# Row scores over 64 contraction rows on two halves of the array, and a tap buffer of its own in the convolution

## The chip, the cores and the metric

The kernel runs on one core of a Trainium2 chip. The metric is device time in microseconds (us) of one execution. Before the change it is 1879.77 us, the median of three runs (1877.68 to 1879.78).

## The reference

Two transformer layers with modulated layer norms run over 4 batches of 1024 rows of 256 values, all in float32. The first layer is a gated long convolution and a feed-forward part with binarised weights. The second is grouped attention and a mixture of two experts. Cut to what matters here:

```
up = u @ in_w + in_b                         # 768 channels
uc = depthwise convolution of up, 3 taps, + short_b
x0, x1, v = uc[:, :256], uc[:, 256:512], uc[:, 512:]
vx = v * x1                                  # then the long convolution of vx, times x0, @ out_w
...
q, k = rope(h @ Wq), rope(h @ Wk)            # 16 query heads, 4 key heads, 64 values each
scores = q k^T / 8, causal mask              # per head 1024 x 1024
out = softmax(scores) @ v
```

## The kernel before, in words

The program is written by hand for each engine; every engine runs its own list of instructions and waits on semaphores. After a setup it handles the 4 batches one after another with the same code. There is no planner: the order on each engine is the order of the loops, and transfers are issued mostly by SyncE (SP).

**Attention.** The float32 operands are split into a high part and a low part (`fp32r`). `qhh` holds the high part of a head's queries twice, in partitions 0 to 63 and 64 to 127. `khl` holds the high part of the keys in partitions 0 to 63 and their low part in 64 to 127. So one matmul over 128 contraction rows gives q_high times (k_high + k_low). The missing q_low times k_high comes from `q2` and `k2`, which hold q_low and k_high in partitions 0 to 63. Their partition 64 holds the negated row maxima and ones, so that the maximum is subtracted by the same matmul of 65 rows.

A head needs its row maxima before its exponentials. `score_rows(u, i)` (L591) computes the scores of 128 query rows of head u against all keys up to the diagonal, in PSUM: (i+1)*128 columns, in one matmul where they fit in 512 and else in two, each with its own weight load. `row_maxima` (L1239, VectorE) reduces them. Eight such tiles make a head: 12 matmuls and 4608 columns. `turn_maxima` (L598) turns the maxima into a row, ScalarE copies it (L927), and SP copies it into `q2` (L1678).

The main loop (L787 to L798) runs over 16 heads of 12 blocks (c, j). In a block TensorE issues `score_cols` (L611, L613, and on diagonal blocks the causal mask L617), then the row tiles that `rows_at` gives, then `values` of four blocks ago (L631, L632, L634). Row tiles 4 to 7 of the next head stand at blocks 0 to 3, one in each, and row tiles 0 to 3 of the head after it at blocks 8 to 11, one in each. Head 1 is computed in head 0, two tiles in each of blocks 0 to 3. Head 0 has its row tiles ahead of the loop. ScalarE takes two exponentials of each block (L942, L943), VectorE or GpSimd the low part (L1249, L1509). PSUM banks 2 to 7 go round among score blocks and row tiles.

**Convolution stage.** For six channel tiles in `E_ORDER` (v0, x1 of 0, v1, x1 of 1, x0 of 0 and 1), TensorE projects (`up_rows`, L450) and ScalarE writes the first tap (L976). GpSimd corrects two edge columns (L1534) and VectorE adds the other two taps (L1327, L1330). There is one buffer `x1` for both x1 tiles. So the second x1 tile (step n == 3) may be written only when v0 has been multiplied with the first; GpSimd does that at n == 1 (L1537). VectorE multiplies v1 with the second x1 tile at n == 3 (L1335). `gated_rows` transposes the products on TensorE (L642), and `spectra` (L661) goes on from them.

GpSimd fills constants for attention (L1556 to L1563) between the last layer norm of the stage before and the first rotation `rotate(0)` (L1516).

Of the kernel before, what the change touches and what calls it, by code (L numbers as in the profile page):

```python
# [60 lines left out]
def rows_at(u, n):  # L61

    if u == 0 and n < 4:
        rows = [(1, 2 * n), (1, 2 * n + 1)]
    elif n < 4:
        rows = [(u + 1, AHEAD + n)]
    else:
        rows = [(u + 2, n - 8)] if n >= 8 else []
    return [(w, i) for w, i in rows if w < HEADS]
# [17 lines left out]
        "w1_split": 2, "x_done": 1, "tap_made": 1, "edge_done": 6, "gates_mixed": 1, "bias_added": 6, "y_pool": 3,  # L87
        "causal_made": 1, "rope_done": 9, "v_done": 4, "low_pool": 112, "x_loaded": 16,
        "gates_loaded": 16, "first_rows0": 64, "first_cols": 64, "first_rows1": 64, "m_loaded0": 128,
# [39 lines left out]
def adaln_hyena_binffn_gqa_moe(nc, d, out, gate_scratch, kf_scratch, q_scratch, k_scratch, inverse_scratch, scratch):  # L129
    es = ExitStack()  # L130
    with es:
# [94 lines left out]
        with ExitStack() as a:  # L226
            with ExitStack() as a3:
                oT = sb("oT", [P, HEADS * HD // P, L], F32, a3)
                qhh = sb("qhh", [P, QRING, L], F32R, a3)
                q2 = sb("q2", [HD + 1, 2, L], F32R, a3)  # L230
                khl = sb("khl", [P, 2, L], F32R, a3)
                k2 = sb("k2", [HD + 1, 2, L], F32R, a3)
                vhi = sb("vhi", [P, KV, NT, HD + 1], F32R, a3)
                vlo = sb("vlo", [P, KV, NT, HD + 1], F32R, a3)
                psplit = sb("psplit", [P, PRING, 2, HALF], F32R, a3)
                pT = sb("pT", [P, FRING - 1, HALF], F32, a3)
                causal = sb("causal", [P, P], F32R, a3)
                mx = sb("mx", [P, 2, NT], F32, a3)
                nm = sb("nm", [P, 2, NT], F32, a3)
                nmr = sb("nmr", [NT, 2, P], F32R, a3)  # L240
                den = sb("den", [P, 2, NT], F32, a3)
                rden = sb("rden", [P, 2, NT], F32, a3)
# [58 lines left out]
        def load_next(dma, h):  # L301

            cols = slice(h * HALF, (h + 1) * HALF)
            one = flat_split(2 * h + 1)[32:HD]
            for half in (0, HD):
                dma(qhh[half:half + HD, 1, cols].bitcast(F32), one[:, 0:2])\
                    .then_inc(q_loaded(1)[0] if h else s["next_loaded"], 16)
            dma(q2[0:HD, 1, cols].bitcast(F32), one[:, 2:4])\
                .then_inc(q2_loaded(1)[0] if h else s["next_loaded"], 16)
# [15 lines left out]
                 "m_loaded1", "v_copied",  # L325
                 "exp_done", "causal_made", "low_pool", "low_dve", "pv_done", "o_done", "sum_loaded", "inverse_done",
                 "inverse_stored", "inverse_loaded", "oT_done", "top_done", "w1_loaded0", "w1_loaded1",
# [105 lines left out]
        def tapped(e):  # L433

            return {0: x0[:, e % ND, :], 1: x1[:, :], 2: vx[:, e % ND, :]}[e // ND]

# [4 lines left out]
        def _(pe):  # L441
# [135 lines left out]
            def score_rows(u, i):  # L577

                g, r, n = u // GQ, u % QRING, (i + 1) * P
                b = bk.take(pe, ("rows", u, i), 1 if n <= HALF else 2)  # L580
                if u == 0 and i % 4 == 0:
                    pe.wait_ge(*at(f"first_rows{i // 4}", 16 * 4))
                elif u and i == 0:
                    if u == 1:
                        pe.wait_ge(*at("next_loaded", 16 * 3))
                    pe.wait_ge(*q_loaded(u))
                    if u % GQ == 0:
                        pe.wait_ge(*k_loaded(g))
                for c in range(0, n, HALF):
                    e = min(n, c + HALF)  # L590
                    q = mm(ps[:, b + c // HALF, 0:e - c], qhh[:, r, i * P:(i + 1) * P], khl[:, g % 2, c:e],  # L591
                           start=True, stop=True)
                q.then_inc(ready[b], 1)
# [135 lines left out]
            for bi in range(B):  # L729
# [5 lines left out]
                for n, e in enumerate(E_ORDER):  # L735
                    if n == 4:
                        gated_rows(0)
                    up_rows(n, e)
# [113 lines left out]
        def _(act):  # L852
# [112 lines left out]
            for bi in range(B):  # L965
                begin(bi)
                act.wait_ge(*at("tap_made", 1))
                for n, e in enumerate(E_ORDER):
                    if n == 5:
                        gated_rows(0)  # L970
                    if n == 3:
                        act.wait_ge(*at("vx_done", 1))
                    dst = tapped(e)
# [72 lines left out]
        def _(dve):  # L1046
# [269 lines left out]
            for bi in range(B):  # L1316
# [4 lines left out]
                for n, e in enumerate(E_ORDER):  # L1321
# [9 lines left out]
                                           in1=dst[:, 2:L], op0=ALU.mult, op1=ALU.add).then_inc(s["conv_done"], 1)  # L1331
                    if n == 3:
                        dve.drain()
                        dve.wait_ge(*at("vx_done", 1))
                        V.tensor_tensor(vx[:, 1, :], vx[:, 1, :], x1[:, :], ALU.mult).then_inc(s["vx_done"], 1)  # L1335

# [121 lines left out]
        def _(pool):  # L1458
# [69 lines left out]
            for bi in range(B):  # L1528
                begin(bi)
                pool.drain().then_inc(s["tap_made"], 1)  # L1530
                for n, e in enumerate(E_ORDER):
                    pool.wait_ge(*at("tap_done", NHALF * n + 1))
                    v = tapped(e)[:, 0:2]
                    G.tensor_tensor(v, v, edge[:, e, :], ALU.add).then_inc(s["edge_done"], 1)  # L1534
                    if n == 1:
                        pool.wait_ge(*at("conv_done", 2))
                        G.tensor_tensor(vx[:, 0, :], vx[:, 0, :], x1[:, :], ALU.mult).then_inc(s["vx_done"], 1)  # L1537
                pool.wait_ge(*at("gates_loaded", 16))
# [23 lines left out]
                pool.drain()  # L1562
                G.memset(k2[HD:HD + 1, :, :].bitcast(F32), 1.0)  # L1563
                pool.drain()
                pool.wait_ge(*at("h_lo_done", (LN_ATT + 1) * NHALF * ND))
                for k in range(3):
# [33 lines left out]
        def _(sp):  # L1600
# [42 lines left out]
            for bi in range(B):  # L1643
# [12 lines left out]
                def load_key(g, cols, done):  # L1656
# [3 lines left out]
                    dma(khl[HD:P, g % 2, cols].bitcast(F32), one[:, 2:4]).then_inc(done, 16)  # L1660
                    dma(k2[0:HD, g % 2, cols].bitcast(F32), one[:, 0:2]).then_inc(done, 16)

# [7 lines left out]
                def load_query_low(u):  # L1670

                    one = q_scratch[u // GQ % 2, u % GQ * 32:(u % GQ + 1) * 32]
                    dma(q2[0:HD, u % 2, :].bitcast(F32), one[:, 2:4]).then_inc(q2_loaded(u)[0], 16)

                def load_maxima(u):

                    sp.wait_ge(*at("nmr_done", u + 1))
                    dma(q2[HD:HD + 1, u % 2, :].bitcast(F32), nmr[:, u % 2, :].bitcast(F32))\  # L1678
                        .then_inc(m_loaded(u)[0], 16)
# [28 lines left out]
                for h, cols in enumerate(half_of):  # L1708
                    dma(k2[0:HD, 0, cols].bitcast(F32), key[h][:, 0:2]).then_inc(s["first_cols"], 16)
                    dma(q2[0:HD, 0, cols].bitcast(F32), query[h][:, 2:4]).then_inc(s["first_cols"], 16)  # L1710
                load_next(dma, 0)
                load_maxima(0)
                store_rest(dma, sp, 2)
# [119 lines left out]
```

## Time and profile before

| | |
|---|---|
| median of three runs | 1879.77 us |
| the profiled execution | 1884.41 us, span 1882.6 us |
| TensorE busy | 1764.5 us (94%) |
| VectorE busy | 1431.3 us (76%) |
| ScalarE busy | 1000.6 us (53%) |
| GpSimd busy | 695.8 us (37%) |
| mean granted TensorE clock | 0.968 |

The profile is of one execution. Busy is the time in which an engine had an instruction in its records. Matmuls overlap in them, so the pace of a stream is read from the starts and not from the durations. PEld is the weight load, PE the matmul. Waits are put down to what released them last.

### The profile page before, as it was taken

The numbers are of one execution on the slowest core, as the hardware profiler recorded it, in microseconds if no ns is written. First come the engines' busy times: TensorE is split into PE (matmuls) and PEld (weight loads), VectorE is DVE, ScalarE is ACT, GpSimd is POOL, SyncE is SP. The second block draws the span as 40 slices with busy tenths as digits, with TensorE's granted clock in tenths as the row PEclk, the third lists the DMA queues.
The fourth block names the chain that finished last, engine by engine and source line by source line (L and its number), as shares of the span: only waits on it lengthen the run. The fifth ranks groups of instructions, "written<-read, shape, count | busy, mean of one in ns | idle before, by whom it ended". The sixth has DMA issues, their size and how long they took to land.

```text
span 1882.6 us, 27319 instructions
## 1 busy us (share of the span) xinstructions
PE 1764.5 (94%) x9228; PEld 1427.0 (76%) x9228; DVE 1431.3 (76%) x2646; ACT 1000.6 (53%) x2162; POOL 695.8 (37%) x725
## 2 busy tenths in 40 slices
PE   8999799999998889999999979999999897999998
PEld 5778577778877767777877867777787785777787
DVE  6788778875678878887468877887656887788754
ACT  2314477676333356777441436777824244777752
POOL 1041444543231344444224144554323324445322
PEclk8999899999999989999999979999999998999999
DMA  7500534432610064343160044444143006354311
GB/s 282 195 7 1 134 108 130 130 69 52 230 56 1 20 168 117 91 133 76 53 250 1 1 118 124 114 102 109 45 169 129 0 1 173 86 135 124 75 30 51
DMA packets 89103, 183.09 MB, mean 97 GB/s; under 512 B 28991, under 2 KB 42111, under 8 KB 85894
## 3 DMA queue, kind: packets, MB, share of 16 engines
q1 hardware_dynamic: 84512, 169.55, 31.1%
q10 hardware_dynamic: 4454, 11.81, 2.0%
q8 instruction: 75, 1.23, 0.3%
q14 instruction: 62, 0.51, 0.1%
HBM read 124.41 MB, written 46.94 MB: 91 GB/s over the span
## 4 chain that ended last, share of the span: by engine, by line
PE 65%; DVE 13%; issue 6%; ACT 5%; DMA 3%; POOL 3%; DVEq 2%; ACTq 2%; SPq 0%; POOLq 0%
PE ps L450 10%; PE ps L591 7%; PE ps L611 7%; PE ps L613 6%; PE ps L634 6%; PE ps L631 6%; PE ps L632 6%; PE ps L804 4%; PE ps L725 3%; PE ps L456 3%; PE ps L680 3%; DVE oT L1260 2%; DVE psplit L1249 2%; PE ps L617 2%; PE ps L548 1%
## 5 line engine op out<-in xcount | busy, mean ns | idle before, releaser
L1239 DVE CUSTOM_DVE_ANT_0 ps<-ps,mrow 128x128 f32<-128x128 f32 (+7 forms) x512 | 385.4, 765 | 104.6 <-PE ps L591 103.0
L1509 POOL TENSOR_TENSOR psplit<-pT,psplit 128x384 fp32r<-128x384 f32 (+3 forms) x320 | 301.9, 957 | 422.6 <-ACT psplit L943 417.5
L943 ACT ACTIVATE psplit<-ps 128x512 fp32r<-128x512 f32 (+3 forms) x768 | 373.0, 486 | 0.0
L942 ACT ACTIVATE pT<-ps 128x512 f32<-128x512 f32 (+3 forms) x512 | 256.2, 500 | 174.0 <-PE ps L617 94.0
L591 PE MATMUL ps<-khl,qhh 128*128 128x512 f32 (+3 forms) x768 | 252.1, 393 | 39.1 <-DMA qhh<-psplit 25.0
L611 PE MATMUL ps<-qhh,khl 128*128 128x512 f32 (+3 forms) x768 | 270.7, 352 | 6.5 <-DMA q<-nmr 6.1
L613 PE MATMUL ps<-q,k 65*128 65x512 f32 (+3 forms) x768 | 268.0, 349 | 0.0
L631 PE MATMUL ps<-psplit,vhi 128*65 128x512 f32 (+3 forms) x768 | 264.2, 344 | 0.0
L634 PE MATMUL ps<-psplit,vhi 128*65 128x512 f32 (+3 forms) x768 | 259.5, 338 | 0.0
L632 PE MATMUL ps<-psplit,vlo 128*65 128x512 f32 (+3 forms) x768 | 259.0, 337 | 0.0
L611 PEld LDWEIGHTS ps<-qhh,khl 128*128 128x128 f32 x768 | 145.3, 189 | 58.3 <-issue 8.7
L591 PEld LDWEIGHTS ps<-khl,qhh 128*128 128x128 f32 x768 | 132.4, 202 | 57.0 <-issue 36.2
L1249 DVE TENSOR_TENSOR psplit<-pT,psplit 128x512 fp32r<-128x512 f32 x192 | 131.1, 707 | 42.3 <-ACT psplit L943 41.4
L942 ACT ACTIVATE mix<-ps 128x512 f32<-128x512 f32 (+2 forms) x256 | 118.1, 461 | 78.2 <-PE ps L613 46.4
L613 PEld LDWEIGHTS ps<-q,k 65*128 65x128 f32 x768 | 145.7, 190 | 17.0
L634 PEld LDWEIGHTS ps<-psplit,vhi 128*65 128x65 f32 x768 | 104.2, 136 | 43.1 <-issue 0.4
L1249 DVE TENSOR_TENSOR psplit<-mix,psplit 128x512 fp32r<-128x512 f32 x128 | 101.5, 793 | 42.1 <-ACT psplit L943 42.1
L632 PEld LDWEIGHTS ps<-psplit,vlo 128*65 128x65 f32 x768 | 104.7, 136 | 34.9
L898 ACT ACTIVATE work<-ps,modb 128x512 f32<-128x512 f32 x48 | 37.3, 778 | 173.5 <-PE ps L548 173.5
L450 PE MATMUL ps<-hT,wqkv 128*128 128x512 f32 x480 | 123.4, 411 | 6.2 <-DVE hT L1150 6.2
L631 PEld LDWEIGHTS ps<-psplit,vhi 128*65 128x65 f32 x768 | 105.5, 137 | 28.5 <-issue 0.3
L1260 DVE TENSOR_TENSOR oT<-work,mix 64x1024 f32<-64x1024 f32 x64 | 94.3, 1474 | 40.5 <-DMA mix<-inverse_scratch 39.6
(211 smaller groups left out, 3302.3 us busy)
## 6 DMA issues: line engine op xcount, KB each, us to landing
qhh<-q_scratch SPq DMA_DIRECT2D x112, 256.0 KB, 5.1
q_scratch<-hrow SPq DMA_DIRECT2D x24, 1024.0 KB, 6.9
mix<-inverse_scratch SPq DMA_DIRECT2D x64, 256.0 KB, 3.5
q<-q_scratch SPq DMA_DIRECT2D x56, 256.0 KB, 4.4
Kf<-kf_scratch SPq DMA_DIRECT2D x3, 3072.0 KB, 17.6
khl<-k_scratch SPq DMA_DIRECT2D x24, 256.0 KB, 7.5
sgn<-sgn_scratch SPq DMA_DIRECT2D x6, 1024.0 KB, 10.7
in_w<-in_w_scratch SPq DMA_DIRECT2D x3, 1536.0 KB, 6.7
```

The costliest lines, as they stand in the source:

```text
L450: i = mm(o, lhs(a, q), rhs(c, q), start=n == 0, stop=n == len(pairs) - 1)
L591: q = mm(ps[:, b + c // HALF, 0:e - c], qhh[:, r, i * P:(i + 1) * P], khl[:, g % 2, c:e], start=True, stop=True)
L611: mm(ps[:, b, 0:hi - lo], khl[:, g % 2, j * P:(j + 1) * P], qhh[:, r, lo:hi], start=True, stop=False)
L613: i = mm(ps[:, b, 0:hi - lo], k2[:, g % 2, j * P:(j + 1) * P], q2[:, u % 2, lo:hi], start=False, stop=not diagonal)
L631: mm(o, vhi[:, g, j, :], high, start=j == 0, stop=False)
L632: mm(o, vlo[:, g, j, :], high, start=False, stop=False)
L634: mm(o, vhi[:, g, j, :], low, start=False, stop=j == 4 * c + 3).then_inc(s["pv_done"], 1)
L942: A(full(n)[:, 0:hi - lo], ps[:, b, 0:hi - lo], ACT.Exp, scale=SCALE)
L943: A(psplit[:, n % PRING, 0, 0:hi - lo], ps[:, b, 0:hi - lo], ACT.Exp, scale=SCALE)\
L1239: V.tensor_tensor_reduce(out=v, in0=v, in1=mrow[:, L - n:L], scale=1.0, scalar=-3e38, op0=ALU.add, op1=ALU.max, accum_out=mx[:, u % 2, i:i ...
L1249: V.tensor_tensor(psplit[:, n % PRING, 1, 0:m], full(n)[:, 0:m], psplit[:, n % PRING, 0, 0:m].bitcast(F32), ALU.subtract)\
L1509: G.tensor_tensor(psplit[:, n % PRING, 1, 0:m], full(n)[:, 0:m], psplit[:, n % PRING, 0, 0:m].bitcast(F32), ALU.subtract)\
```

## The change

The row scores of heads 1 to 15 contract 64 rows, the high parts alone, and no longer add k_low. Head 0 is as before. One matmul uses partitions 0 to 63 of `qhh` and `khl`, the other partitions 64 to 127 of `qhh` and of `k2`. For this `k2` and `q2` move to partitions 64 to 127 and are 128 partitions tall. The maxima and the ones are in partition 0, and partitions 1 to 63 are zero, so the matmul L613 contracts 128 rows. Row tiles of more than 512 columns put the first 512 keys on the lower half and the rest on the upper; shorter ones go by turns, tile by tile. Row tiles 0 to 3 are now issued as two pairs, at blocks 8 and 10. GpSimd clears `q2` and `k2`, and SP waits for it (`pads_made`) before the first copy of maxima.

In the convolution stage the second x1 tile is written to `work[:, 0:2]`. ScalarE's wait for `vx_done` goes. GpSimd makes both products, at n == 2 and n == 4, and TensorE issues `gated_rows(0)` at n == 5 instead of n == 4.

```diff
@@ rows_at
-        rows = [(u + 2, n - 8)] if n >= 8 else []
+        rows = [(u + 2, n - 8), (u + 2, n - 7)] if n in (8, 10) else []
@@ buffers
-                q2 = sb("q2", [HD + 1, 2, L], F32R, a3)
+                q2 = sb("q2", [P, 2, L], F32R, a3)
-                k2 = sb("k2", [HD + 1, 2, L], F32R, a3)
+                k2 = sb("k2", [P, 2, L], F32R, a3)
@@ tapped
-            return {0: x0[:, e % ND, :], 1: x1[:, :], 2: vx[:, e % ND, :]}[e // ND]
+            if e // ND == 1:
+                return x1[:, :] if e % ND == 0 else work[:, 0:2, :].rearrange("p a n -> p (a n)")
+            return (x0 if e // ND == 0 else vx)[:, e % ND, :]
@@ score_rows
-                    q = mm(ps[:, b + c // HALF, 0:e - c], qhh[:, r, i * P:(i + 1) * P], khl[:, g % 2, c:e],
-                           start=True, stop=True)
+                    if u == 0:
+                        rows_of, keys = slice(0, P), khl
+                    elif (c // HALF if n > HALF else i % 2) == 0:
+                        rows_of, keys = slice(0, HD), khl
+                    else:
+                        rows_of, keys = slice(HD, P), k2
+                    q = mm(ps[:, b + c // HALF, 0:e - c], qhh[rows_of, r, i * P:(i + 1) * P],
+                           keys[rows_of, g % 2, c:e], start=True, stop=True)
@@ TensorE, convolution stage
-                    if n == 4:
+                    if n == 5:
                         gated_rows(0)
@@ ScalarE, convolution stage
-                    if n == 3:
-                        act.wait_ge(*at("vx_done", 1))
@@ VectorE, convolution stage
-                    if n == 3:
-                        dve.drain()
-                        dve.wait_ge(*at("vx_done", 1))
-                        V.tensor_tensor(vx[:, 1, :], vx[:, 1, :], x1[:, :], ALU.mult).then_inc(s["vx_done"], 1)
@@ GpSimd, convolution stage
-                    if n == 1:
-                        pool.wait_ge(*at("conv_done", 2))
-                        G.tensor_tensor(vx[:, 0, :], vx[:, 0, :], x1[:, :], ALU.mult).then_inc(s["vx_done"], 1)
+                    if n in (2, 4):
+                        pool.wait_ge(*at("conv_done", n))
+                        dt = n // 4
+                        G.tensor_tensor(vx[:, dt, :], vx[:, dt, :], tapped(ND + dt), ALU.mult).then_inc(s["vx_done"], 1)
@@ GpSimd, constants
-                G.memset(k2[HD:HD + 1, :, :].bitcast(F32), 1.0)
+                G.memset(q2[0:HD, :, :].bitcast(F32), 0.0)
+                G.memset(k2[0:HD, :, :].bitcast(F32), 0.0)
                 pool.drain()
+                G.memset(k2[0:1, :, :].bitcast(F32), 1.0)
+                pool.drain().then_inc(s["pads_made"], 1)
@@ SP
-                    dma(q2[HD:HD + 1, u % 2, :].bitcast(F32), nmr[:, u % 2, :].bitcast(F32))\
+                    dma(q2[0:1, u % 2, :].bitcast(F32), nmr[:, u % 2, :].bitcast(F32))\
...
+                sp.wait_ge(*at("pads_made", 1))
                 load_maxima(0)
```

The other transfers into `q2` and `k2` go to partitions 64 to 127 instead of 0 to 63; their number, sizes and order stay.

## Rows read from the trace of the kernel before

**Rows 1.** The page, busy us of TensorE (share of the span), instructions.

```profile
PE 1764.5 (94%) x9228; PEld 1427.0 (76%) x9228; DVE 1431.3 (76%) x2646; ACT 1000.6 (53%) x2162; POOL 695.8 (37%) x725
```

**Rows 2.** Windows, attention loop of batch 0: length, PE, PEld, DVE, ACT, POOL busy, clock, DMA.

```profile
220.30:458.00 237.70, 235.80 (x1314) 185.95 (x1315) 189.20 (x376) 174.68 (x427) 112.00 (x121) 0.99 0.41 105
```

**Rows 3.** Chain that ended last, 380 to 460 us, shares by line.

```profile
by line: PE ps L611 16.2%; PE ps L613 15.6%; PE ps L634 14.8%; PE ps L632 14.8%; PE ps L591 14.7%; PE ps L631 14.5%; PE ps L617 4.1%; DVE psplit L1249 2.9%; DVE oT L1260 1.5%; PE ps L598 0.7%; issue 0.4%; ACT psplit L943 0.3%; ACTq L941 0.0
```

**Rows 4.** Timeline, PE, one head: start, us, line, names, rows x columns, count.

```profile
422.71 0.22 PE L617 MATMUL ps<-causal,identr 128*128 128x128 f32 x1
422.77 0.51 PE L591 MATMUL ps<-khl,qhh 128*128 128x512 f32 x2
423.12 0.40 PE L631 MATMUL ps<-psplit,vhi 128*65 128x512 f32 x1
...
426.56 0.68 PE L591 MATMUL ps<-khl,qhh 128*128 128x512 f32 x2
427.07 0.22 PE L631 MATMUL ps<-psplit,vhi 128*65 128x128 f32 x1
...
431.73 0.28 PE L591 MATMUL ps<-khl,qhh 128*128 128x128 f32 x1
431.85 0.40 PE L631 MATMUL ps<-psplit,vhi 128*65 128x512 f32 x1
...
435.33 0.45 PE L591 MATMUL ps<-khl,qhh 128*128 128x512 f32 x1
435.61 0.39 PE L631 MATMUL ps<-psplit,vhi 128*65 128x512 f32 x1
```

**Rows 5.** Timeline, setup: matmuls (PE) and the weight loads (PEld) that follow them.

```profile
16.02 2.76 PE L497 MATMUL ps<-sine,fw 64*64 64x512 f32 x3
...
16.87 0.23 PEld L497 LDWEIGHTS ps<-sine,fw 64*64 64x64 f32 x1 [0.62 <-issue]
18.71 1.14 PEld L472 LDWEIGHTS ps<-cT,spare 128*128 128x128 f32 x5 [1.61 <-issue]
...
32.73 3.63 PE L472 MATMUL ps<-cT,Kf 128*128 128x4 f32 x32
...
36.29 5.41 PEld L532 LDWEIGHTS ps<-fwo,sine 64*128 64x128 f32 x16
...
27.82 5.07 PE L525 MATMUL ps<-w2T,ones 128*128 128x256 f32 x16
...
32.52 3.76 PEld L472 LDWEIGHTS ps<-cT,Kf 128*128 128x128 f32 x32
```

**Rows 6.** Timeline, PE, a matmul whose weight load starts with it.

```profile
427.34 0.50 PE L611 MATMUL ps<-qhh,khl 128*128 128x512 f32 x1
427.68 0.40 PE L613 MATMUL ps<-q,k 65*128 65x512 f32 x1
```

**Rows 7.** Timeline of the convolution stage, batch 1, and one window of it.

```profile
530.40 2.38 POOL L1537 TENSOR_TENSOR vx<-vx,x 128x1024 f32<-128x1024 f32 x1 [3.90 <-DVE x L1330]
...
533.07 1.28 DVE L1327 SCALAR_TENSOR_TENSOR vx<-ps,short_w,vx 128x1023 f32<-128x1023 f32 x1 [2.75 <-POOL vx L1534]
...
535.76 7.35 PE L450 MATMUL ps<-hT,in_w 128*128 128x512 f32 x24 [1.83 <-DVE vx L1330]
...
535.70:538.50 2.80, 2.74 (x7) 2.16 (x8) 2.63 (x4) 0.00 (x0) 0.00 (x0) 0.51 0.00 0
```

**Rows 8.** Timeline, GpSimd's constants and VectorE's layer norm, batches 0 and 1.

```profile
185.09 0.20 POOL L1556 MEMSET causal<- 128x128 f32 x1
...
185.18 1.44 DVE L1141 TENSOR_SCALAR hrow<-x,mv,rstd 128x256 f32<-128x256 f32 x4 [1.12 <-POOL rstd L1475]
...
636.99 1.80 POOL L1563 MEMSET k<- 1x2048 f32 x1
642.96 1.30 POOL L1516 TENSOR_TENSOR oT<-oT 128x512 f32<-128x512 f32 x1 [4.17 <-DVE hT L1150]
...
635.95 2.99 DVE L1141 TENSOR_SCALAR hrow<-x,mv,rstd 128x256 f32<-128x256 f32 x4 [1.12 <-POOL rstd L1475]
```

More of the change, by code:

```diff
@@ L87 @@
         "w1_split": 2, "x_done": 1, "tap_made": 1, "edge_done": 6, "gates_mixed": 1, "bias_added": 6, "y_pool": 3,
-        "causal_made": 1, "rope_done": 9, "v_done": 4, "low_pool": 112, "x_loaded": 16,
+        "causal_made": 1, "pads_made": 1, "rope_done": 9, "v_done": 4, "low_pool": 112, "x_loaded": 16,
         "gates_loaded": 16, "first_rows0": 64, "first_cols": 64, "first_rows1": 64, "m_loaded0": 128,
@@ L307, in load_next @@
                     .then_inc(q_loaded(1)[0] if h else s["next_loaded"], 16)
-            dma(q2[0:HD, 1, cols].bitcast(F32), one[:, 2:4])\
+            dma(q2[HD:P, 1, cols].bitcast(F32), one[:, 2:4])\
                 .then_inc(q2_loaded(1)[0] if h else s["next_loaded"], 16)
@@ L325, in adaln_hyena_binffn_gqa_moe @@
                  "m_loaded1", "v_copied",
-                 "exp_done", "causal_made", "low_pool", "low_dve", "pv_done", "o_done", "sum_loaded", "inverse_done",
+                 "exp_done", "causal_made", "pads_made", "low_pool", "low_dve", "pv_done", "o_done", "sum_loaded", "inverse_done",
                  "inverse_stored", "inverse_loaded", "oT_done", "top_done", "w1_loaded0", "w1_loaded1",
@@ L1660, in load_key @@
                     dma(khl[HD:P, g % 2, cols].bitcast(F32), one[:, 2:4]).then_inc(done, 16)
-                    dma(k2[0:HD, g % 2, cols].bitcast(F32), one[:, 0:2]).then_inc(done, 16)
+                    dma(k2[HD:P, g % 2, cols].bitcast(F32), one[:, 0:2]).then_inc(done, 16)
                 def load_query(u):
@@ L1672, in load_query_low @@
                     one = q_scratch[u // GQ % 2, u % GQ * 32:(u % GQ + 1) * 32]
-                    dma(q2[0:HD, u % 2, :].bitcast(F32), one[:, 2:4]).then_inc(q2_loaded(u)[0], 16)
+                    dma(q2[HD:P, u % 2, :].bitcast(F32), one[:, 2:4]).then_inc(q2_loaded(u)[0], 16)
                 def load_maxima(u):
                     sp.wait_ge(*at("nmr_done", u + 1))
-                    dma(q2[HD:HD + 1, u % 2, :].bitcast(F32), nmr[:, u % 2, :].bitcast(F32))\
+                    dma(q2[0:1, u % 2, :].bitcast(F32), nmr[:, u % 2, :].bitcast(F32))\
                         .then_inc(m_loaded(u)[0], 16)
@@ L1708, in _ @@
                 for h, cols in enumerate(half_of):
-                    dma(k2[0:HD, 0, cols].bitcast(F32), key[h][:, 0:2]).then_inc(s["first_cols"], 16)
-                    dma(q2[0:HD, 0, cols].bitcast(F32), query[h][:, 2:4]).then_inc(s["first_cols"], 16)
+                    dma(k2[HD:P, 0, cols].bitcast(F32), key[h][:, 0:2]).then_inc(s["first_cols"], 16)
+                    dma(q2[HD:P, 0, cols].bitcast(F32), query[h][:, 2:4]).then_inc(s["first_cols"], 16)
                 load_next(dma, 0)
+                sp.wait_ge(*at("pads_made", 1))
                 load_maxima(0)
```

## The prediction, made before the kernel ran

> **What bounds the kernel now.** I read the page first: TensorE is busy in 94% of the span, far above the rest [rows 1]. Next come the windows of each engine over the four attention loops. The first is 237.7 us long, and four such are half of the span. In it TensorE is busy in 99%, VectorE in 80% and ScalarE in 73%, at nearly the full clock [rows 2]. Then the chain of waits inside a loop: nine tenths of it are TensorE's matmuls one behind the other, and the row scores L591 hold 14.7% [rows 3]. So in the loop a saved microsecond of TensorE is a microsecond of the kernel, and so is an added one. Last I read the timeline of one head for the price of row scores by the starts of what stands around them. Row tile 4 holds TensorE for 423.12 - 422.77 = 0.35 us, row tile 7 for 427.07 - 426.56 = 0.51, row tile 0 for 0.12 and row tile 3 for 0.28 [rows 4]. The tiles between lie evenly between these ends (each 128 columns add some 0.06), so the eight are 0.12 + 0.17 + 0.23 + 0.28 + 0.35 + 0.40 + 0.46 + 0.51 = 2.52 us a head. Columns pass at 0.23 us for 512.
>
> **Row scores, the streams.** The number of matmuls and of columns stays. What may come down is the time, if the two halves of the array stream at once. Then a tile of more than 512 columns lasts as long as its lower 512 keys, 0.23 us; the pair of tiles 0 and 1 lasts 0.12 and the pair of 2 and 3 lasts 0.23. That is 4 x 0.23 + 0.12 + 0.23 = 1.28 us a head, half of now. No row shows two halves at work, so I bound it: between these 1.28 us and the 2.52 of now. I take overlap of the streams. Each half has weights of its own, though. A load of 128 columns that isn't hidden costs 0.11 us: L611 at 427.34, whose load starts with it, holds TensorE for 0.34 instead of 0.23 [rows 6]. If the loads of the two halves follow each other, the upper half starts 0.11 later and the six groups last 0.23 + 0.23 + 0.29 + 0.34 + 0.23 + 0.34 = 1.66 us.
>
> **Row scores, the change of shape.** In the loop every weight load is hidden behind the matmul before it. The setup shows that this ends where the number of contraction rows changes between 64 and 128. After L497 (64 rows) the last matmul ends at 16.02 + 2.76 = 18.78, and the load of L472 (128 rows) starts at 18.71. The loads inside L497 follow at the pace of the matmuls (16.87 stands 0.85 behind 16.02), so this one would have come at 17.72, with the start of the last matmul. In the other direction L472 ends at 36.36 and the load of L532 starts at 36.29. Both times the load waits until 0.07 before the end of the recorded matmul. Where both have 128 rows it doesn't wait: L525 ends at 32.89, and the load of L472 started at 32.52, 0.37 before it [rows 5]. A 512-column matmul in the loop is recorded for 0.39 and passes in 0.23, so its record ends 0.16 after its stream, and a load at 0.07 before that comes 0.09 after the stream. L497 at half the pace would give 18.71 - (17.72 + 0.85) = 0.14. I take 0.09.
>
> So each group of row scores between L617 and L631 pays 0.09 + 0.11 going in and 0.09 + 0.06 coming out (the 65 columns of `vhi` load in half of 0.11): 0.35 us. In a head there are six groups, at blocks 0 to 3, 8 and 10: 2.10 us. With the streams a head's row scores take 2.10 + 1.28 = 3.38 to 2.10 + 1.66 = 3.76 us against 2.52, so 0.86 to 1.24 more; I take 1.05. Heads 2 to 15 of four batches are 56: 59 us. Head 1 has four groups (1.40) and streams of 1.66: 3.06 against 2.52, so 0.5 x 4 = 2 us. Together **+61 us**, between 56 x 0.86 = +48 and 56 x 1.24 + 2 = +72 while the halves overlap. All of it lies on the path, since TensorE has no free time in the loop. VectorE gets its row tiles later and has a fifth of its time free [rows 2]; the pairs at blocks 8 and 10 only move its work by a block.
>
> The Trainium skill speaks against this change in "TensorEngine Tiling (Array Packing)", Key Properties: going over to another tiling mode drains TensorE. It gives no time for it; this trace agrees, with the 0.07 us above, though in setup code and float32.
>
> **L613 with 128 rows instead of 65: nothing.** 65 rows x 512 columns are recorded for 0.40, as are 128 rows (L631) [rows 4, 6]. I bound it at 0 to 0.01 us for each of 768, so 0 to 8 us, and take 0.
>
> **PSUM banks and semaphores: nothing.** A pair takes two banks at once instead of one in each of two blocks. VectorE must have reduced them before six more banks are taken, over 3 us later. Without that cover the price would be a stall of a reduction, up to 0.7 us a head; TensorE slowed by the groups widens the cover.
>
> **Convolution stage.** Now VectorE ends the taps of step 1 at 530.3 and starts step 2 at 533.07, after 2.75 us of waiting for GpSimd's product (2.38 us), behind which the edge of step 2 stands. TensorE's step 4 waits for the banks of step 2 until 535.76 [rows 7]. After the change the edge stands ahead of the product, so VectorE goes on at once. Step 2 is done at 533.1, and TensorE's step 4 starts 2.7 us earlier. Step 3 waits for no product any more, but GpSimd's edge of step 3 is behind the first product: ready at 530.4 + 2.38 + 0.2 = 533.0, as VectorE needs it. VectorE's product (1.2 us) goes to GpSimd at 2.4 us, from 535.8 to 538.2, and the last transposes need it only behind step 5, near 540. The edge of step 5 is behind it and needed at about 540 as well. If GpSimd is slower beside a busy VectorE, up to 0.8 us come back. TensorE's transposes move behind step 4. TensorE stands still ahead of step 4 before and after, so the 0.51 clock there (the 1.2 GHz level) stays. I take -2.7 x 4 = **-11 us**, between -7 and -12.
>
> **Clearing `q2` and `k2`.** The fill of one row of 2048 takes 1.80 us. I take the same for 64 rows, since a fill of 128 rows x 128 takes 0.20, no more than its columns ask for; there are three instead of one, +3.6 us on GpSimd. It runs from 637.0 to 642.4, and its next work starts at 643.0, so that part is hidden in most batches. But VectorE's layer norm lasts 2.99 us instead of 1.44 where the fill falls on it [rows 8], in two of the four batches, and TensorE's transposes wait for it. A second fill may hold it again: 0 to 1.8 in each batch. I take **+3 us**, between 0 and 6. SP's new wait for `pads_made` costs nothing: behind the fills and ahead of the first `load_maxima` stand the rotations, all row scores of head 0 and their maxima. If it did bind, SP's two stores behind it and the first `score_cols` would wait.
>
> **The sum.** 61 - 11 + 3 = +53 us on the profiled execution's 1884.4: 1937. The median is 4.6 us lower than that execution, so **1933 us**. This case's own range is 1905 to 1955: the bounds of the terms give +36 to +74, and a shorter wait at the full clock (0.05 instead of 0.09, twice in each of 336 groups) takes 27 off.
>
> **Rivals.**
> *A, the halves overlap and no load waits.* Then the loads are pulled ahead as now. With all hidden a head saves 2.52 - 1.28 = 1.24 us. Where both loads of 0.11 must pass behind the short L617 (0.06), a group begins 0.11 to 0.16 late and it is about 0.55. So -33 to -74 us over 60 heads, with -8 for the rest -41 to -82; near the middle **1820 us**. For it: every load in the loop is hidden now. Against it: the two changes of shape in the setup. It decides for faster once the price of a group falls under (2.52 - 1.66) / 6 = 0.14 us. The Trainium skill holds for it in "TensorE: Matmul & The Clock Gate", Part 3: tiles in different row groups load and stream at once, with some 4 ns between starts. By that page alone the result would be this rival's; no row here shows it.
> *B, neither overlap nor waiting.* Row scores cost what they do, and the convolution remains: -8, **1872 us**. For it: the three matmuls of L497 with 64 rows run one by one, though they all use the same rows. Against it: the waiting loads [rows 5].
> *C, waiting but no overlap.* 2.10 us more in 56 heads, 1.4 in four: +123 - 8 = +115, **1995 us**. For it: no row shows an overlap.
>
> **How the numbers follow.** Forecast 0.52, A 0.20, B 0.06, C 0.12; the rest, 0.10, is a group price of about half, with +5 to +25 us, 1885 to 1905. What a measurement here can tell from no change is about 0.2%, 4 us. Faster: A, B and a little of the rest, 0.28. Same: 0.04. Slower: 0.68. The range reaches from 1820, which takes in half of A, to 1965.
>
> **What would show it.** Right: in a head of the changed kernel the start of L631 stands 0.6 us or more behind L617 at blocks 0 to 3, against 0.41 now at block 0; the load of the row scores starts 0.15 behind L617 instead of with it; loops of about 252 us instead of 237 [rows 2]; step 4 of the convolution 2.7 us earlier against step 0. Wrong: loads of L591 that start during L617, and loops under 237 us; then the waiting in rows 5 belongs to plain float32 or to the setup.

## The result, and the profile after

The changed kernel takes 1900.7 us in the median of four runs (1898.86 to 1903.7), the kernel before 1879.24 beside it (1877.68 to 1879.78). The ratio is 1.0117, with a 95% interval of 1.01 to 1.0135: slower by 21.5 us, where +53 was forecast. The profiled execution took 1902.25 us around a span of 1900.5, against 1882.6 before, so the traces have 17.9 us to explain. Times below are of fast executions; one execution of experiment 4 took 4343.54 us, in a slow state, and is left out.

The page of the changed kernel, busy time by engine, against [rows 1]:

```profile
PE 1787.3 (94%) x9228; PEld 1370.6 (72%) x9228; DVE 1430.9 (75%) x2642; ACT 1004.2 (53%) x2162; POOL 720.5 (38%) x737
```

TensorE has 23 us more of busy time for the same 9228 matmuls, and weight loading has 56 less. The window over the attention loop of batch 0 (length, then PE, PEld, DVE, ACT, POOL, clock, DMA), against [rows 2]:

```profile
217.00:467.00 250.00, 246.08 (x1324) 175.01 (x1325) 191.89 (x379) 176.78 (x430) 112.61 (x121) 0.99 0.37 100
```

The loop is longer at the same mean clock (0.99), and VectorE and ScalarE have about the busy time that they had. The ends of the first loop are the first and the last start of the score columns. The group by line of the kernel before, then of the kernel after (medians in ns, then the first start and the last):

```profile
L611 PE MATMUL ps<-qhh,khl x192: 220/388/507, 220.3 to 459.9; 128*128 128x512 f32 x96, 128*128 128x384 f32 x32, 128*128 128x256 f32 x32, 128*128 128x128 f32 x32
```

```profile
L619 PE MATMUL ps<-qhh,khl x192: 218/389/793, 217.6 to 467.4; 128*128 128x512 f32 x96, 128*128 128x384 f32 x32, 128*128 128x256 f32 x32, 128*128 128x128 f32 x32
```

239.6 us became 249.8. Read to 0.1 us, the same distance grew by 10.2, 10.1, 4.0 and 7.6 us in the four batches: +31.9 together. From the last score matmul of a batch to the first matmul behind the next convolution it shrank by 3.3, 3.7, 3.0 and 2.9: -12.9. From there to the loop it changed by +0.6, -0.1, +0.3 and -2.0: -1.2; the fills stand in this stretch. With +0.1 at the tail this is the 17.9.

**One group of row scores.** The timeline of the changed kernel, TensorE, a head's blocks 0 and 3 (row tiles 4 and 7), to be read beside [rows 4]:

```profile
429.25 0.22 PE L625 MATMUL ps<-causal,identr 128*128 128x128 f32 x1
429.40 0.50 PE L599 MATMUL ps<-khl,qhh 64*128 64x512 f32 x1
429.40 0.32 PE L599 MATMUL ps<-k,qhh 64*128 64x128 f32 x1
429.83 0.44 PE L639 MATMUL ps<-psplit,vhi 128*65 128x512 f32 x1
430.11 0.39 PE L640 MATMUL ps<-psplit,vlo 128*65 128x512 f32 x1
...
433.48 0.27 PE L625 MATMUL ps<-causal,identr 128*128 128x128 f32 x1
433.69 0.49 PE L599 MATMUL ps<-khl,qhh 64*128 64x512 f32 x1
433.69 0.49 PE L599 MATMUL ps<-k,qhh 64*128 64x512 f32 x1
434.11 0.27 PE L639 MATMUL ps<-psplit,vhi 128*65 128x128 f32 x1
```

And the weight loads of the first of them:

```profile
429.01 0.19 PEld L625 LDWEIGHTS ps<-causal,identr 128*128 128x128 f32 x1
429.40 0.18 PEld L599 LDWEIGHTS ps<-khl,qhh 64*128 64x128 f32 x1 [0.20 <-issue]
429.40 0.18 PEld L599 LDWEIGHTS ps<-k,qhh 64*128 64x128 f32 x1
429.83 0.13 PEld L639 LDWEIGHTS ps<-psplit,vhi 128*65 128x65 f32 x1 [0.24 <-issue]
```

The halves overlap: with 512 columns on each, the group at 433.69 is as long (0.42) as that at 429.40 with 512 and 128 (0.43). The load isn't pulled ahead: it starts 0.15 behind L625, which streams for 0.06, so 0.09 is waiting. From there L639 is 0.43 away: 0.11 of load, 0.23 of stream and 0.09 of waiting. L640 follows L639 by 0.28, which is 0.05 more than a stream, for the load of 65 columns. These are the forecast's 0.09 + 0.11 + 0.09 + 0.06, where the 0.20 beside the stream is measured as a whole and its split into load and waiting is the forecast's. The two loads of L599, however, start in the same moment. The Trainium skill, "TensorE: Matmul & The Clock Gate", Part 3, gives some 4 ns between the starts of tiles in different row groups; the trace agrees within its 0.01 us, for the loads and for the two matmuls (429.40 each).

**The convolution** of the changed kernel, batch 1, timeline, beside [rows 7]:

```profile
528.23 11.20 PE L452 MATMUL ps<-hT,in_w 128*128 128x512 f32 x48
...
540.31 3.06 PE L452 MATMUL ps<-hT,in_w 128*128 128x512 f32 x12 [0.89 <-DVE vx L1336]
...
537.61 1.28 DVE L1333 SCALAR_TENSOR_TENSOR vx<-ps,short_w,vx 128x1023 f32<-128x1023 f32 x1
...
536.24 0.20 POOL L1536 TENSOR_TENSOR vx<-vx,edge 128x2 f32<-128x2 f32 x1 [2.52 <-ACT vx L982]
537.61 2.39 POOL L1540 TENSOR_TENSOR vx<-vx,x 128x1024 f32<-128x1024 f32 x1 [1.18 <-DVE x L1336]
```

The edge (536.24) is ahead of the product, and VectorE starts step 2 together with the product, without the 2.75 us of idle time. TensorE's step 4 starts 12.08 us behind its first matmul of the stage (540.31 - 528.23). In the kernel before, the same distance was 14.74 (535.76 less the start at 521.02): -2.66.

### The profile page after: what moved, and what is told of

Its sections match the earlier page's. It is cut to its first block, busy times and chain, and to the rows that moved or that the text cites. A ratio compares the mean times of both kernels' runs of the same rounds, so it can differ in the third digit from the quotient of the medians.

```text
span 1900.5 us, 27327 instructions
## 1 busy us (share of the span) xinstructions
PE 1787.3 (94%) x9228; PEld 1370.6 (72%) x9228; DVE 1430.9 (75%) x2642; ACT 1004.2 (53%) x2162; POOL 720.5 (38%) x737
## 4 chain that ended last, share of the span: by engine, by line
PE 68%; DVE 13%; issue 6%; DVEq 3%; DMA 3%; ACT 3%; ACTq 2%; POOL 2%; POOLq 0%; SPq 0%
PE ps L452 10%; PE ps L639 9%; PE ps L619 7%; PE ps L621 7%; PE ps L642 6%; PE ps L640 6%; PE ps L599 6%; PE ps L812 4%; PE ps L733 3%; DVE psplit L1255 2%; PE ps L625 2%; PE ps L688 2%; DVE ps L1245 2%; DVE oT L1266 1%; PE ps L458 1%
## 5 line engine op out<-in xcount | busy, mean ns | idle before, releaser
L1245 DVE CUSTOM_DVE_ANT_0 ps<-ps,mrow 128x128 f32<-128x128 f32 (+7 forms) x512 | 381.6, 770 | 127.0 <-PE ps L599 124.0
L1511 POOL TENSOR_TENSOR psplit<-pT,psplit 128x384 fp32r<-128x384 f32 (+3 forms) x320 | 309.0, 975 | 442.1 <-ACT psplit L951 442.1
L639 PE MATMUL ps<-psplit,vhi 128*65 128x512 f32 (+3 forms) x768 | 281.6, 367 | 0.0
L621 PE MATMUL ps<-q,k 128*128 128x512 f32 (+3 forms) x768 | 267.6, 348 | 0.0
L642 PE MATMUL ps<-psplit,vhi 128*65 128x512 f32 (+3 forms) x768 | 259.4, 338 | 0.0
L640 PE MATMUL ps<-psplit,vlo 128*65 128x512 f32 (+3 forms) x768 | 258.7, 337 | 0.0
L599 PE MATMUL ps<-khl,qhh 64*128 64x512 f32 (+6 forms) x408 | 183.7, 472 | 39.2 <-DMA qhh<-psplit 26.1
L619 PEld LDWEIGHTS ps<-qhh,khl 128*128 128x128 f32 x768 | 145.0, 189 | 58.1 <-DVE mx L1245 10.1
L639 PEld LDWEIGHTS ps<-psplit,vhi 128*65 128x65 f32 x768 | 103.7, 135 | 93.8 <-issue 65.3
L621 PEld LDWEIGHTS ps<-q,k 128*128 128x128 f32 x768 | 145.7, 190 | 15.4
L599 PE MATMUL ps<-k,qhh 64*128 64x256 f32 x360 | 152.0, 422 | 0.0
L599 PEld LDWEIGHTS ps<-khl,qhh 64*128 64x128 f32 (+1 forms) x408 | 78.7, 200 | 89.3 <-issue 45.5
L1255 DVE TENSOR_TENSOR psplit<-mix,psplit 128x512 fp32r<-128x512 f32 x128 | 106.7, 834 | 42.0 <-ACT psplit L951 42.0
L452 PE MATMUL ps<-hT,wqkv 128*128 128x512 f32 x480 | 128.0, 422 | 6.2 <-DVE hT L1156 6.2
## 6 DMA issues: line engine op xcount, KB each, us to landing
Kf<-kf_scratch SPq DMA_DIRECT2D x3, 3072.0 KB, 17.5
```

The costliest lines, as they stand in the source:

```text
L452: i = mm(o, lhs(a, q), rhs(c, q), start=n == 0, stop=n == len(pairs) - 1)
L599: q = mm(ps[:, b + c // HALF, 0:e - c], qhh[rows_of, r, i * P:(i + 1) * P], keys[rows_of, g % 2, c:e], start=True, stop=True)
L619: mm(ps[:, b, 0:hi - lo], khl[:, g % 2, j * P:(j + 1) * P], qhh[:, r, lo:hi], start=True, stop=False)
L621: i = mm(ps[:, b, 0:hi - lo], k2[:, g % 2, j * P:(j + 1) * P], q2[:, u % 2, lo:hi], start=False, stop=not diagonal)
L639: mm(o, vhi[:, g, j, :], high, start=j == 0, stop=False)
L640: mm(o, vlo[:, g, j, :], high, start=False, stop=False)
```

## The experiments

In the text below, "a head" is the distance from one head's transposes of the maxima to the next head's, within batch 0, and it has the number of the transposes that it begins with, counted from 0. Plain heads are those with neither a projection nor a load in the way: 14.04 to 14.07 us before, 14.70 to 14.72 after. One of each, before and then after:

```profile
416.00 0.27 PE L598 MATMUL ps<-identr,nm 128*8 128x128 f32 x1
430.05 0.27 PE L598 MATMUL ps<-identr,nm 128*8 128x128 f32 x1
```

```profile
437.00 0.27 PE L606 MATMUL ps<-identr,nm 128*8 128x128 f32 x1
451.69 0.27 PE L606 MATMUL ps<-identr,nm 128*8 128x128 f32 x1
```

**1. The convolution part alone**, on the kernel before.

```diff
@@ TensorE
-                    if n == 4:
+                    if n == 5:
                         gated_rows(0)
@@ GpSimd (and tapped(), and the lines taken from ScalarE and VectorE, as in the change)
-                    if n == 1:
-                        pool.wait_ge(*at("conv_done", 2))
-                        G.tensor_tensor(vx[:, 0, :], vx[:, 0, :], x1[:, :], ALU.mult).then_inc(s["vx_done"], 1)
+                    if n in (2, 4):
+                        pool.wait_ge(*at("conv_done", n))
+                        dt = n // 4
+                        G.tensor_tensor(vx[:, dt, :], vx[:, dt, :], tapped(ND + dt), ALU.mult).then_inc(s["vx_done"], 1)
```

> The kernel before with the convolution part of the change alone. Theory (the three parts add up, and the row scores cost more than the whole change shows): about 13 us faster than before, since the spans from the last score matmul of a batch to the first transform of the next are 3.0 to 3.7 us shorter in the changed kernel; near 1867 us. Rival (the convolution gains nothing by itself, the spans are shorter only because of how the loop before them ends): 1879 us, no change.

Measured: 1866.24 us, ratio 0.9919 (0.9895 to 0.9943): 14.1 us faster. Plain heads stay at 14.05. The other half of the change:

**2. The row scores and fills without the convolution part.** The changed kernel with those lines of the convolution stage put back.

```diff
-                    if n == 5:
+                    if n == 4:
                         gated_rows(0)
...
-                    if n in (2, 4):
+                    if n == 1:
...
```

> The kernel before with the row-score part of the change and its fills, without the convolution part. Theory (the parts add up): the changed kernel's 21 us plus the 14 us that the convolution part gives alone, 35 us above before, 1915 us. Rival (the convolution part gives less beside the row scores, or the row scores cost less alone): 1900 to 1908 us.

Measured: 1913.18 us, ratio 1.0176 (1.0153 to 1.0199), so +32.2. The parts add up to +18.1 against the +21.5 of both, a difference that these intervals (some 4 us either way) hold.

**3. The new order of the groups, but 128 rows.** The placement of the changed kernel, with row scores that contract over high and low parts as before.

```diff
-                    if u == 0:
+                    if True:
```

> The changed kernel with all row scores over 128 rows again (q_high times k_high + k_low); the pairs at blocks 8 and 10, the tall q2 and k2, their fills and the convolution stay. Theory (the loss is in the change between 64 and 128 rows): same as the convolution part alone, 1865 to 1871 us. Rival (pairs, 128 rows in L613 or the fills cost part of the loss): 1875 to 1890 us.

Measured: 1870.54 us, ratio 0.9941 (0.9918 to 0.9964). Plain heads 13.96 (444.38 - 430.42), 0.74 under the changed kernel's. So the slowdown comes from the 64-row matmuls, some 30 us of them. The pairs, the fills and the taller `q2` and `k2` together make no more than the 4.3 us between this kernel and that of experiment 1, which the intervals just hold. The pairs do two things in the traces: plain heads get 0.09 shorter than before, and heads 4 and 8 get 0.55 longer (18.09 against 17.54), with a new wait for VectorE.

**4. All on one half.** 64 rows everywhere, but every key on partitions 0 to 63.

```diff
-                    elif (c // HALF if n > HALF else i % 2) == 0:
+                    elif True:
```

> The changed kernel with every 64-row matmul of the row scores on the lower half of the array, so that none can overlap; same six groups a head. Theory (a group has a fixed price of 0.32 us, and what overlaps is the streams, 2.10 us of columns against 1.28): 0.82 us more a head, 60 heads, 49 us above the changed kernel, near 1950 us. Rival (the halves gain nothing, the price of a group is smaller): 1900 us as the changed kernel.

Measured: 1943.85 us, the median of three runs, ratio 1.0341 (1.0302 to 1.038). Timeline of its TensorE, block 0, two matmuls (512 and 128 columns) in one row:

```profile
449.90 0.22 PE L625 MATMUL ps<-causal,identr 128*128 128x128 f32 x1
450.05 0.56 PE L599 MATMUL ps<-khl,qhh 64*128 64x512 f32 x2
450.54 0.45 PE L639 MATMUL ps<-psplit,vhi 128*65 128x512 f32 x1
```

The waits are the same (0.15 behind L625), and the group lasts 0.49 instead of 0.43: the 128 columns now stand behind the 512. A head is 15.59 (458.23 - 442.64), 0.89 more than after, where the streams that no longer overlap make 0.79: 4608 columns at 0.23 for 512 are 2.07 us one by one, and 1.28 on two halves; the other 0.10 was not traced. So the overlap is real, and the waiting needs neither the upper half nor two halves at once.

**5. Eight groups instead of six.**

```diff
-        rows = [(u + 2, n - 8), (u + 2, n - 7)] if n in (8, 10) else []
+        rows = [(u + 2, n - 8)] if n >= 8 else []
```

> The changed kernel with tiles 0 to 3 alone again, one at each of blocks 8 to 11, so eight groups a head instead of six and no pair of short tiles. Theory (0.35 us for a group, loads of the two halves at once): two groups more are 0.70 us, and the short streams one by one are 0.06 + 0.12 + 0.17 + 0.23 = 0.58 instead of 0.35, so 0.93 us a head more than the changed kernel: plain heads of 15.63 us, near 1950 us. Rival (the price goes by matmul or by column): heads of 14.9 us, near 1915 us.

Measured: 1937.54 us, ratio 1.031 (1.0277 to 1.0343), heads of 15.61. Of the 0.91 more, 0.23 are streams that the pairs overlapped, so two groups cost 0.68: 0.34 each.

**6. Three groups.**

```diff
-        rows = [(u + 1, AHEAD + n)]
+        rows = [(u + 1, AHEAD + n), (u + 1, AHEAD + n + 1)] if n in (0, 2) else []
     else:
-        rows = [(u + 2, n - 8), (u + 2, n - 7)] if n in (8, 10) else []
+        rows = [(u + 2, i) for i in range(4)] if n == 9 else []
```

> The changed kernel with the same row matmuls on both halves in three groups a head instead of six: tiles 4 and 5 at block 0, 6 and 7 at block 2, 0 to 3 at block 9. Theory (fixed price of a group 0.32 us): 3 x 0.32 x 56 heads and a little in head 1's four, 54 us less than the changed kernel, 1845 us, which beats the kernel before; head 1 keeps its four groups. Rival (price by matmul and not by group, or VectorE's larger clumps of reductions hold the PSUM banks): 1880 to 1905 us.

Measured: 1863.39 us, ratio 0.99 (0.9868 to 0.9931): 37 us under the changed kernel, not the 54 expected. Its transposes of the maxima, from one plain head to the next, and in the second pair behind a projection:

```profile
301.71 0.27 PE L606 MATMUL ps<-identr,nm 128*8 128x128 f32 x1
316.15 0.27 PE L606 MATMUL ps<-identr,nm 128*8 128x128 f32 x1
...
432.83 0.27 PE L606 MATMUL ps<-identr,nm 128*8 128x128 f32 x1
446.49 0.27 PE L606 MATMUL ps<-identr,nm 128*8 128x128 f32 x1
```

The later pair is the plain one, 13.66: three groups fewer take off 1.04, or 0.35 each. The earlier pair (head 5) takes 14.44. New waits stand in head 1 (242.05) and head 5 (309.28), in the same kernel's timeline:

```profile
242.05 0.50 PE L619 MATMUL ps<-qhh,khl 128*128 128x512 f32 x1 [0.48 <-DVE mx L1245]
...
309.28 0.46 PE L599 MATMUL ps<-khl,qhh 64*128 64x512 f32 x1 [0.36 <-DVE mx L1245]
```

Clumps of two and four row tiles need banks that VectorE's reductions (L1245) still hold. The expectation priced the groups rightly and left this wait out.

**7. Three groups and less on VectorE.** One block's low part of the probabilities goes from VectorE to GpSimd.

```diff
-DVE_LOW = BLOCKS[4:9]
+DVE_LOW = BLOCKS[5:9]
```

> The three groups with one low part of each head, block (1, 0), moved from VectorE to GpSimd. Theory (what three_groups lost of its 54 us is TensorE waiting for banks that VectorE frees late, above all in heads 2, 5 and 9): those heads get 0.5 to 1.3 us shorter, 8 to 12 us in all, 1853 us. Rival (GpSimd's low parts come late for values, or the waits are of another kind): no gain or slower than 1863 us.

Measured: 1856.64 us, ratio 0.9867 (0.9838 to 0.9897). Head 1 falls from 15.05 (250.31 - 235.26) to 13.80, head 5 from 14.44 to 14.07 (314.71 - 300.64), and plain heads stay at 13.66. So VectorE was behind nearly all of the wait in head 1 and half of that in head 5; the wait of 0.36 for L1245 in head 5 stays. The whole time, 7 us less, is at the edge of what the two intervals can tell apart.

**8. The same move of a low part on the convolution-only kernel.**

```diff
@@ on the kernel of experiment 1
-DVE_LOW = BLOCKS[4:9]
+DVE_LOW = BLOCKS[5:9]
```

> The convolution part alone with the same low part moved to GpSimd. Theory: TensorE waits for VectorE in only two heads of a batch (0.8 us each) and a little in each other one, so up to 6 us less than the convolution part alone: 1860 to 1866 us. Rival (GpSimd becomes late): slower than 1866 us.

Measured: 1859.17 us, ratio 0.9888 (0.9858 to 0.9919). Plain heads remain at 14.05; heads 5 and 9 go from 14.82 to 14.43, and heads 4 and 8 from 17.5 to 17.15. So the kernel before already had waits in these heads, in heads 5 and 9 0.8 us over a plain one, and VectorE's work is behind half of that.

**9. Three groups with 128 rows.** Experiments 3 and 6 together.

```diff
-                    if u == 0:
+                    if True:
...
+        rows = [(u + 1, AHEAD + n), (u + 1, AHEAD + n + 1)] if n in (0, 2) else []
+        rows = [(u + 2, i) for i in range(4)] if n == 9 else []
```

> The three clumps of row tiles (blocks 0, 2 and 9) with all row scores over 128 rows. Theory (three changes of shape cost 1.05 us, half the streams save 1.24, so 64 rows are worth little here): plain heads of 13.9 to 14.0 us against 13.66 with 64 rows, 1865 to 1875 us. Rival (the gain of the three groups comes from where the tiles stand): plain heads of 13.7 us and the same time as three_groups, 1863 us.

Measured: 1867.12 us, ratio 0.9928 (0.9901 to 0.9956), plain heads 13.71 (439.21 - 425.50). That is 0.2 under what was expected, and 0.05 from the 64-row head of experiment 6: in the heads the rival of the expectation held. In three groups the halves of the array bring next to nothing. Clumping shortens plain heads of 128 rows as well, by 0.25 against experiment 3.

**10. The convolution part, three groups of 128 rows and the moved low part**, without any 64-row matmul, tall `q2` or fill.

```diff
@@ on the kernel of experiment 8
+        rows = [(u + 1, AHEAD + n), (u + 1, AHEAD + n + 1)] if n in (0, 2) else []
+        rows = [(u + 2, i) for i in range(4)] if n == 9 else []
```

> The convolution part, row tiles of 128 rows in three clumps a head (blocks 0, 2 and 9), one low part moved to GpSimd; no 64-row matmul, no tall q2 and k2. Theory (clumps hide the weight loads of the row tiles, so that 4608 columns cost little over their 2.10 us): plain heads of 13.7 us as in three_order, and without VectorE's waits about 1855 us, as good as the best with 64 rows or better. Rival (64 rows are worth their three changes of shape once VectorE is relieved): 1862 us or more, behind three_pool's 1857.

Measured: 1857.69 us, ratio 0.9873 (0.9851 to 0.9895). It equals experiment 7 within the intervals. Both beat the kernel before by 1.3% and the changed one by 2.3%. But experiment 8, with neither 64 rows nor clumps, took 1859.17 (ratio 0.9888, 0.9858 to 0.9919), and that can't be told from either. Plain heads are 13.79 here against its 14.05, so the clumps show in the heads and not in the whole time. What is shown to pay in the whole time is the convolution part; the moved low part shows in heads 4, 5, 8 and 9.

## Why the prediction was right in sign and wrong in size

**The step that failed** is the term for the row scores: "Heads 2 to 15 of four batches are 56: 59 us", +61 together. The loops measured +31.9. Its mechanism held, its price per group too: forecast 0.35, measured 0.34 (eight against six groups) and 0.35 (six against three). Three things were mis-sized, and they make 61 - 10.6 - 7.8 - 10.1 = 32.5. The convolution's term had a wrong step as well, and a wait for banks was put at nothing; both stand further down.

*The loads of the two halves.* I let them follow each other and took 1.05 a head, the middle between 0.86 and 1.24. They start together, so 0.86 is right: 0.19 x 56 = 10.6 us. The lower bound of the term was the value to take once overlap of the streams was assumed; I had no reason for a middle.

*Heads with slack of their own.* I charged all 56 heads. Heads 5 and 9 of each batch, behind a projection, had waits for other engines in them: 14.82 before and 14.70 after, while a plain head went from 14.05 to 14.70. So the changed kernel's longer groups fall into time that was lost anyway. Transposes of the maxima of head 5, of the kernel before and of the one after:

```profile
295.84 0.27 PE L598 MATMUL ps<-identr,nm 128*8 128x128 f32 x1
310.66 0.27 PE L598 MATMUL ps<-identr,nm 128*8 128x128 f32 x1
```

```profile
298.45 0.27 PE L606 MATMUL ps<-identr,nm 128*8 128x128 f32 x1
313.15 0.27 PE L606 MATMUL ps<-identr,nm 128*8 128x128 f32 x1
```

Eight such heads at -0.12 instead of +0.86 make 7.8 us. Experiment 8 shows whose the slack was: half of it goes when VectorE has less to do. The other half stays there, and its wait is put down to ScalarE's exponentials, as in this row of the kernel before:

```profile
306.00 0.68 PE L591 MATMUL ps<-khl,qhh 128*128 128x512 f32 x2 [0.21 <-ACT psplit L943]
```

"TensorE has no free time in the loop" was an average over the loop that I took for every head.

*A loss of the kernel before that vanished.* A plain head grew by 0.65 and not by 0.86. The distances from L617 to L632 (from L625 to L640 after) over the eight blocks sum to 4.62 before and 5.45 after, +0.83 where 0.86 was priced. The rest of the gain lies outside them, and 0.13 of it in one place: behind the last short value matmul of block 3. Timeline of the kernel before, the head behind that of [rows 4], and its load:

```profile
441.25 0.22 PE L634 MATMUL ps<-psplit,vhi 128*65 128x128 f32 x1
441.40 0.50 PE L611 MATMUL ps<-qhh,khl 128*128 128x512 f32 x1
441.75 0.39 PE L613 MATMUL ps<-q,k 65*128 65x512 f32 x1
441.97 0.39 PE L631 MATMUL ps<-psplit,vhi 128*65 128x512 f32 x1
...
441.20 0.14 PEld L634 LDWEIGHTS ps<-psplit,vhi 128*65 128x65 f32 x1
441.40 0.19 PEld L611 LDWEIGHTS ps<-qhh,khl 128*128 128x128 f32 x1
```

And of the changed kernel, the same place:

```profile
448.98 0.22 PE L642 MATMUL ps<-psplit,vhi 128*65 128x128 f32 x1
449.04 0.45 PE L619 MATMUL ps<-qhh,khl 128*128 128x512 f32 x1
449.33 0.40 PE L621 MATMUL ps<-q,k 128*128 128x512 f32 x1
449.57 0.39 PE L639 MATMUL ps<-psplit,vhi 128*65 128x512 f32 x1
...
448.93 0.14 PEld L642 LDWEIGHTS ps<-psplit,vhi 128*65 128x65 f32 x1
448.99 0.19 PEld L619 LDWEIGHTS ps<-qhh,khl 128*128 128x128 f32 x1
```

L634 to L631 is 0.72 before, and 0.59 after: before, the load of L611 starts 0.15 behind L634 and with its own matmul, as [rows 6] showed. I had read those rows as the price of an unhidden load, and not asked why it was unhidden there. The 0.14 to 0.15 stands there in every kernel whose row tile 7 comes alone with 128 rows (before, experiments 1, 3 and 8), and 0.06 in those with 64 rows and in both clumped ones with 128. Why that load isn't pulled ahead stays open, as do the last 0.05 of a head. Together it is 0.21 x 48 = 10.1 us, with all 48 heads taken as plain.

That 32.5 comes so near to 31.9 is luck. Heads 0 and 3 of each batch, with a projection in them, are 16 to 21 us long and vary by 1.5 to 2.8 us from batch to batch in either kernel. Where TensorE's clock falls after a wait, a head 3 is longer: in the kernel before 18.29 us at a granted clock of 1.00 in batch 0, and 20.53 at 0.92 in batch 2. This makes the scatter of the four loops (+4.0 to +10.2); the loops of experiment 2, with the same row scores, grew by 23.6 and not by 31.9. The other 13 distances of each batch are steady. They grew by 26.8 us in all (776.3 to 803.0), in experiment 2 by 26.7, and 44 x 0.65 - 8 x 0.12 = 27.6 is the account of them.

**What held.** Change of shape: shown above, and the sign of the result hangs on it; rival A (1820) falls with the loads at 429.40, B and C with the overlap at 433.69. VectorE's free fifth in the plain heads: no new wait in the changed kernel. L613 with 128 rows: L621 streams 512 columns in 0.23 to 0.24. SP's wait: nothing. Of the signs, the load of the row scores starts 0.15 behind L625 as said, and L639 stands 0.58 (block 0) to 0.63 (block 3) behind it, where 0.6 or more was said. The measured 1900.7 lies in the band of 1885 to 1905 that the prediction kept for a group price of about half; the price was the full one, so the time fell there for other reasons.

**PSUM banks.** They were put at nothing, with VectorE's cover in a plain head as the reason. In heads 4 and 8, which have a projection in them, the pairs bring a wait that the kernel before doesn't have. Experiment 3 has it too, with 128 rows and 18.09 us a head, so the growth of these heads from 17.54 to 18.15 comes from the pairs and hardly from the 64 rows. Timeline of the changed kernel:

```profile
290.66 0.39 PE L619 MATMUL ps<-qhh,khl 128*128 128x256 f32 x1 [0.37 <-DVE mx L1245]
```

**Convolution.** -11 was forecast, -12.9 measured in the traces and -14.1 by experiment 1; the -2.66 of the step-4 distance is the -2.7 of the forecast. The rest, 0.7 us from the start of step 4 to the last transposes, comes from a step that was wrong: "the 0.51 clock there (the 1.2 GHz level) stays". Windows over this stretch, before and after:

```profile
535.76:542.95 7.19, 7.19 (x24) 5.75 (x25) 5.25 (x5) 3.20 (x5) 0.24 (x2) 0.76 0.00 0
```

```profile
540.31:546.82 6.51, 6.51 (x32) 5.38 (x33) 5.04 (x4) 3.32 (x5) 2.87 (x4) 1.00 0.06 21
```

The mean granted clock is 1.00 and no longer 0.76. Ahead of the stretch TensorE was idle for 0.63 and 1.83 us before, and is for 0.89 now. So the stretch is 0.68 shorter, although the first eight transposes now lie in it. The same holds in batches 2 and 3.

**Fills.** +3 was forecast, and -1.2 was measured around them. The same stretches grew by 3.1 in the trace of experiment 2 and changed by -1.1 in that of experiment 1, so the fills cost nothing that this scatter of some 3 us would let show. Timeline of the changed kernel, GpSimd's constants and VectorE's layer norm in batch 1, beside [rows 8]:

```profile
640.52 1.80 POOL L1566 MEMSET q<- 64x2048 f32 x1
642.27 1.94 POOL L1567 MEMSET k<- 64x2048 f32 x1
644.33 1.80 POOL L1569 MEMSET k<- 1x2048 f32 x1
646.49 1.30 POOL L1518 TENSOR_TENSOR oT<-oT 128x512 f32<-128x512 f32 x1 [0.36 <-DVE hT L1156]
...
639.48 2.99 DVE L1147 TENSOR_SCALAR hrow<-x,mv,rstd 128x256 f32<-128x256 f32 x4 [1.12 <-POOL rstd L1477]
```

64 rows fill as fast as one, as taken. The layer norm is held once, for 2.99 us, as before in this batch, and ends at 642.47, when the second fill has just begun; over the kernel it is held in three batches instead of two. GpSimd is through with its fills 0.36 us before the input of L1518 is there, so they are just hidden.

With the loads together (-10.6), the slack (-7.8), the vanished loss (-10.1), the convolution (-1.9) and the fills (-4.2), the traces' own +18 comes out of the forecast's +53: 53 - 34.6 = 18.4. The terms have the scatter told above, so this shows that nothing large is missing and no more.

## What to carry to other kernels

Half-height matmuls beside full-height ones are priced by the number of changes, 0.35 us for each visit here, against the columns that they save: six visits cost 2.1 us a head, and row scores otherwise fell from 2.52 to 1.28. So gather them until the visits are few, and then ask whether gathering alone, without the half-height, does as well, as it did here (1857.69 against 1856.64 us), and whether even gathering shows in the whole time; here it didn't (1859.17 without it). And when an added cost is multiplied by a count, look for the members of that count that are bound by something else: in a stage at 99% busy a seventh of the heads counted here had 0.8 us of waits for VectorE and ScalarE.

## What the runs showed of the hardware that was not expected

- Weight loads for the two halves of the array start in the same moment (429.40 both) and last no longer together (0.18 us) than one load of 128 rows (0.19), where loads of full height pass at a pace of 0.11 one behind the other (448.99 and 449.10 in the changed kernel).
- The change between 128 and 64 contraction rows is what stops loads from being pulled ahead. The number of weight columns doesn't: L631 follows the 8-column transpose L598 by 0.03 us (430.05, 430.08), and 65 and 128 columns follow each other all through the loop. Nor does 65 rows beside 128: L613 of the kernel before follows L611 by 0.23 where nothing else waits (430.52, 430.75 in the head of [rows 4]).
- GpSimd's fill of 64 rows x 2048 takes 1.80 to 1.94 us, that of one row 1.80; beside busy VectorE its product of 128 x 1024 takes 2.39, as it did without that neighbour [rows 7].
